# Last layer: first chunk's tiles side by side, products ahead of the mixture, second mixture first in a chunk

## The chip, the cores and the metric

The kernel runs on one core of one Trainium2 chip. The metric is the device time of one execution in microseconds (us). The kernel before took 3504.18 us as the median of 3 runs (3500.18 to 3504.94). PE is TensorE, DVE VectorE, ACT ScalarE, POOL GpSimd, SP the engine that issues the DMAs. Times of rows count from the start of the profiled execution's span.

## What is computed

Four residual layers on x of shape (16, 256, 512), 4096 tokens of width 512, all in fp32. The first three (a cross attention, a quantized feed-forward layer, a masked attention) are the same before and after. The fourth is the one that is touched:

```python
def _mole(x, W, b, A, Bm, Rw):
    gates = softmax(einsum('bsd,de->bse', x, Rw))          # 3 experts
    base = einsum('bsd,dh->bsh', x, W) + b
    z = einsum('bsd,edr->ebsr', x, A)                      # rank 8
    zg = z * transpose(gates, (2, 0, 1))[..., None]
    lora = einsum('ebsr,erh->bsh', zg, Bm)
    return base + SCALING * lora

def _L1_ffn_ref(x, W1, b1, A1, B1, R1, W2, b2, A2, B2, R2):
    h = relu(_mole(x, W1, b1, A1, B1, R1))                 # 512 -> 2048
    return _mole(h, W2, b2, A2, B2, R2)                    # 2048 -> 512

x = x + _L1_ffn_ref(_layernorm(x, axis=-1), ...)
```

## The kernel before

The last layer (`lora_ffn`, tile names `lf_`) works on the 4096 tokens in 8 chunks of 512. A chunk is four row tiles of 128 tokens. The engines' queues are written out by hand, one Python function for each engine, and they meet over semaphores. Every engine works through its queue in order, so what stands ahead of an instruction in its queue also holds it up.

**Products.** An fp32 factor is held as two parts, a high part rounded to fp32r and the rest, and `product` (L187 to L189) makes three matmuls of 128x128 by 128x512: high by high, high by low, low by high.

**Head of a chunk.** For each row tile `t`: SP loads it to `xin` (two buffers), DVE takes statistics (`stats`, L2473 and L2475), POOL makes the reciprocal deviation (L2462, L2464), DVE normalises the rows in place (`rows`, L2480), PE turns the tile with four transposes into the PSUM bank `pj` (`turn_tile`, L2644), ACT writes the high part of `xT` (`turned_hi`, L2570) and DVE the low part (`turned_lo`, L2485). There is one bank `pj`, and each job on it waits for the one before. When the four tiles are turned, PE makes the projections to gates and ranks (`first_projections`, eight matmuls, L2653), ACT copies them (`projected`, L2574, to `zT`), PE turns them back (`turn_projections`, L2660), DVE and ACT work out the gates and weigh the ranks (`mixture`, L2492 to L2516, with `exps`, L2578), PE turns the result (`turn_mixture`, L2667) and ACT copies it (`mixed`, L2582, to `mixT`).

**Body of a chunk.** `m` runs over 16 strips of 128 hidden features and two more steps (`LAG` is 2). In step `m` PE makes the strip's twelve main products and the side product with `mixT` (`hidden`, L187 to L189 and L2677) into one of two banks `hb`, ACT and DVE take the two parts of the relu from the bank (L2587, L2522), and two steps later PE uses the strip for the second product (`use_hidden`: two matmuls to `pz`, L2685, and twelve to the four banks `py`). Main products of strip `m` wait until the bank of strip `m - 2` has been read by DVE (`h_done`). The head of the next chunk lies within the body: tiles at `m` = 1 to 9, projections at 10, their turn at 11, the mixture's turn at 16.

**Tail of a chunk.** The second layer's projections of chunk `c - 1` (`pz`, copied by ACT at L2591 to `zT` as the last thing of its body) are handled inside the body of chunk `c`: the turn of the projections behind strip 0, `mixture` behind strip 0's low part on DVE, `exps` behind strip 0's high part on ACT, the turn of the mixture ahead of strip 2, and the side product and the output behind strip 2 (`second_lora`, L2698, `end`, L2528).

**Weights.** The two weight matrices are loaded in 16 pieces of 512 KB during chunk 0, in turn into the two halves of `y`. ACT and DVE split each (`piece_hi`, L2595; `piece_lo`, L2532). Piece `i` may be loaded when piece `i - 2` is split. Strips 0 and 1 need piece 0, strips 2 and 3 piece 1; the second product of strip 0 needs piece 2. Pieces 0 to 3 stand in the head of chunk 0, one behind each row tile, on both engines; piece `m + 4` stands in step `m` of the body. On SP the loads of tiles 2 and 3 of chunk 0 stand between the loads of pieces 1, 2 and 3 and wait until tile 0 or 1 has been turned and read (L2412, L2421).

**Start.** POOL clears `zg` with three memsets before anything else; DVE and PE wait for them first.

## Time and profile before

| | us |
|---|---|
| median of 3 runs | 3504.18 |
| lowest and highest run | 3500.18, 3504.94 |
| the profiled execution | 3504.39 |
| its span, first to last instruction | 3502.7 |
| PE busy in the span | 3225.8 (92%) |
| DVE, ACT, POOL busy | 1919.8, 1557.3, 779.3 |
| last layer, from its first instruction (2581.1) to the span's end | 921.6 |

The profile is one execution. The chain that ended last is PE's through nearly all of the last layer. A matmul's record is longer than the distance to the next one, since matmuls are pipelined; distances are taken between starts. "Granted clock" is the share of full speed that TensorE's throttle gave: 1.00 is 2.4 GHz, 0.50 is 1.2 GHz.

### The profile page before, as it was taken

To read this page: it belongs to the slowest core of one execution; us is meant where nothing else is said; L and a number is where in the kernel's file an instruction comes from. 1 tells how busy PE (TensorE), PEld (TensorE's weight loads), DVE (VectorE), ACT (ScalarE), POOL (GpSimd) and SP (SyncE) were. 2 spreads that over 40 slices of the span, in tenths; PEclk is the share of its full clock that TensorE was granted. 3 is DMA by queue.
4 is the path that set the end of the run, shared out by engine and by line. 5 is a ranking of instruction groups with operands and counts; after the bars stand their busy time and mean duration, and the time that the engine had idled before them with its cause. 6 is when DMAs were issued, how large, how long until landed. Compare 5 with 4: busy or idle time off the path is not lost. (4 is left out here: it accounts for less than half of the span.)

```text
span 3502.7 us, 51565 instructions
## 1 busy us (share of the span) xinstructions
PE 3225.8 (92%) x17304; PEld 2762.2 (79%) x17304; DVE 1919.8 (55%) x3294; ACT 1557.3 (44%) x2948; POOL 779.3 (22%) x1136
## 2 busy tenths in 40 slices
PE   7999979999999979998996787997959999999998
PEld 6989869999999967886885565885847777877776
DVE  3245558888888855556888885554743222122211
ACT  3222257777777743335776775654722111111110
POOL 0000057777777740000000200002710000000000
PEclk9999989999999999999998898998979999999999
DMA  6477754555555426555666675444832100011000
GB/s 184 134 238 235 220 171 148 153 156 165 154 153 159 144 95 243 177 174 174 221 221 218 208 235 200 166 168 148 253 103 84 37 31 19 24 36 37 31 25 12
DMA packets 370165, 503.48 MB, mean 144 GB/s; under 512 B 58940, under 2 KB 237420, under 8 KB 366032
## 3 DMA queue, kind: packets, MB, share of 16 engines
q1 hardware_dynamic: 356746, 475.46, 43.2%
q0 software_dynamic: 4480, 16.78, 1.4%
q10 hardware_dynamic: 8720, 8.41, 0.7%
q8 instruction: 127, 2.08, 0.3%
q14 instruction: 92, 0.75, 0.1%
HBM read 292.86 MB, written 174.11 MB: 133 GB/s over the span
## 5 line engine op out<-in xcount | busy, mean ns | idle before, releaser
L2522 DVE SCALAR_TENSOR_TENSOR lf_hT<-lf_hb,lf_hT 128x512 fp32r<-128x512 f32 x128 | 88.6, 692 | 618.8 <-ACT lf_hT L2587 617.4
L2587 ACT ACTIVATE lf_hT<-lf_hb 128x512 fp32r<-128x512 f32 x128 | 76.8, 600 | 685.1 <-PE lf_py L189 636.4
L770 POOL TENSOR_TENSOR at_prob<-at_prob,at_rec 128x308 f32<-128x308 f32 (+1 forms) x256 | 261.4, 1043 | 199.1 <-DVE at_rec L812 198.9
L906 ACT ACTIVATE at_prob<-at_sc,at_nm 128x77 f32<-128x77 f32 (+1 forms) x1024 | 293.5, 383 | 3.3 <-DVE at_nm L799 3.3
L799 DVE TENSOR_REDUCE at_nm<-at_sc 128x4 f32<-128x308 f32 (+1 forms) x256 | 164.8, 686 | 82.4 <-PE at_sc L960 80.8
L919 ACT ACTIVATE at_pT<-at_tp 128x1024 fp32r<-128x1024 f32 x128 | 131.8, 1030 | 166.7 <-PE at_tp L970 166.6
L187 PE MATMUL lf_hb<-lf_xT,lf_w 128*128 128x512 f32 x512 | 204.8, 400 | 0.0
L189 PE MATMUL lf_hb<-lf_xT,lf_w 128*128 128x512 f32 x512 | 203.7, 398 | 0.0
L189 PE MATMUL lf_py<-lf_w,lf_hT 128*128 128x512 f32 x512 | 203.2, 397 | 0.0
L188 PE MATMUL lf_hb<-lf_xT,lf_w 128*128 128x512 f32 x512 | 203.1, 397 | 0.0
L187 PE MATMUL lf_py<-lf_w,lf_hT 128*128 128x512 f32 x512 | 202.8, 396 | 0.0
L188 PE MATMUL lf_py<-lf_w,lf_hT 128*128 128x512 f32 x512 | 202.3, 395 | 0.0
L187 PE MATMUL dn_py<-qf_wd,dn_om 128*128 128x512 f32 x384 | 150.7, 393 | 25.2 <-DVE dn_om L1874 25.2
L805 DVE TENSOR_REDUCE at_sums<-at_prob 128x4 f32<-128x308 f32 (+1 forms) x256 | 172.9, 676 | 0.0
L816 DVE TENSOR_TENSOR at_pT<-at_tp,at_pT 128x1024 fp32r<-128x1024 f32 x128 | 156.5, 1222 | 29.9 <-ACT at_pT L919 29.9
L187 PE MATMUL pg_bank<-pg_xs,qg_wg 128*128 128x512 f32 x384 | 153.0, 398 | 20.7 <-DVE pg_xs L1369 20.7
L757 POOL TENSOR_TENSOR at_ks<-at_kr,at_ks 128x512 fp32r<-128x512 f32 x128 | 165.3, 1292 | 16.1 <-ACT at_ks L913 16.1
L187 PE MATMUL pu_bank<-pu_xs,qu_wu 128*128 128x512 f32 x384 | 150.8, 393 | 17.4 <-DVE pu_xs L1369 16.9
L2462 POOL TENSOR_SCALAR lf_var<-lf_mv 128x1 f32<-128x1 f32 x32 | 7.1, 223 | 717.4 <-DVE lf_mv L2475 717.4
L187 PE MATMUL at_vq<-at_xT,xo_Wq 128*128 128x256 f32 x512 | 147.0, 287 | 19.3 <-DMA at_xT<-xn_parts 12.7
L187 PE MATMUL at_vq<-at_pT,at_vs 128*128 128x256 f32 x512 | 154.9, 303 | 0.2 <-DVE at_qst L824 0.2
L960 PEld LDWEIGHTS at_sc<-at_ks,at_qs 128*128 128x128 f32 x1024 | 140.4, 192 | 14.2 <-DMA at_qs<-at_qst 4.4
(324 smaller groups left out, 9510.0 us busy)
## 6 DMA issues: line engine op xcount, KB each, us to landing
at_kr<-k_rows SPq DMA_DIRECT2D x256, 128.0 KB, 2.9
at_qs<-at_qst SPq DMA_DIRECT2D x512, 64.0 KB, 2.1
raw_gate<-pg_stage SPq DMA_DIRECT2D x96, 256.0 KB, 2.0
pu_rg<-raw_gate SPq DMA_DIRECT2D x96, 256.0 KB
raw_up<-pu_stage SPq DMA_DIRECT2D x96, 256.0 KB, 2.1
om_raw<-raw_up SPq DMA_DIRECT2D x48, 512.0 KB, 4.3
dn_raw<-raw_up SPq DMA_DIRECT2D x48, 512.0 KB, 3.8
xn_parts<-pr_xturned SPq DMA_DIRECT2D x32, 512.0 KB, 4.8
```

Of the source, the lines that this page charges most:

```text
L187: pe.matmul(out, lh, rh, start=start, stop=False, **kw)
L188: pe.matmul(out, lh, rl, start=False, stop=False, **kw)
L189: return pe.matmul(out, ll, rh, start=False, stop=stop, **kw)
L757: pool.tensor_tensor(ks[:, n % NK, :, 1, :], kr[:, n % NKR], ks[:, n % NK, :, 0, :].bitcast(F32), ALU.subtract).then_inc(k_low, 1)
L770: ins = pool.tensor_tensor(prob[:, i, :, lo:hi], prob[:, i, :, lo:hi], rec[:, z, g, :].unsqueeze(2).broadcast_to([P, 2 * NTE, hi - lo]), A ...
L799: ins = dve.tensor_reduce(nm[:, n % 2, g, :], sc[n % 2][:, :, lo:hi], AX_X, ALU.max, negate=True)
L805: dve.tensor_reduce(sums[:, z, g, :], prob[:, i, :, SEG[g][0]:SEG[g][1]], AX_X, ALU.add).then_inc(sum_done, 1)
L816: dve.tensor_tensor(pT[:, n % 2, 1], tp[:], pT[:, n % 2, 0].bitcast(F32), ALU.subtract).then_inc(pt_done, 1)
L906: ins = act.activation(prob[:, i, m, lo:hi], sc[n % 2][:, m, lo:hi], ACT.Exp, bias=nm[:, n % 2, g, m:m + 1])
L919: act.activation(pT[:, n % 2, 0], tp[:], ACT.Copy).then_inc(pt_hi, 1)
L960: ins = pe.matmul(sc[n % 2][:, h * NTE + m, :], qs[:, n % NQ, h, m * P:(m + 1) * P], ks[:, n % NK, h, part, :], start=part == 0, stop=part ...
L2522: dve.scalar_tensor_tensor(hT[:, i, 1, :], hb[i][:], 0.0, hT[:, i, 0, :].bitcast(F32), ALU.max, ALU.subtract).then_inc(h_done, 1)
```

## The change

Three edits, all in `lora_ffn`.

1. Chunk 0's four row tiles get a place each (`first_rows`: the two `xin` buffers, `zT` and `zg`, which are not in use yet) and a semaphore each for tiles 2 and 3. SP issues the four loads first and then those of pieces 0 to 3. DVE's order is statistics of two tiles, then rows, statistics and low parts overlapped; pieces 0 to 3 are split behind the tiles, except that piece 0 stands between tiles 1 and 2. PE turns each tile into a bank of its own (`py`, not in use yet). POOL's memsets of `zg` come after the four deviations and the four turns, and DVE waits for them only ahead of the first mixture.
2. `hidden` is cut into `hidden_main` (twelve products) and `hidden_side` (the product with `mixT`). In chunk 0 the main products of strip 0 stand behind the projections, those of strip 1 behind the turn of the projections; both side products follow the turn of the mixture.
3. In chunks 1 to 7 the turn of the second projections stands ahead of strip 0 on PE, `mixture` ahead of strip 0's low part on DVE and `exps` ahead of its high part on ACT.

```diff
--- before.py
+++ after.py
@@ -2357,6 +2357,9 @@
         w_high, w_low = ph.sem("w_high"), ph.sem("w_low")
         W1, W2 = a["L1_ffn_W1"], a["L1_ffn_W2"]
         PIECES, EARLY, PC = 2 * (KH // 2), 4, 2 * P
+        first_ready = [ph.sem(f"first_ready{i}") for i in range(2, NT)]
+
+        first_rows = [xin[:, 0, :], xin[:, 1, :], zT[:], zg[:].rearrange("p t n -> p (t n)")]
         block = ph.block()
 
 
@@ -2421,12 +2424,10 @@
                 sp.dma_start(staged(i), piece(i)[0]).then_inc(w_ready[i % 2], 16)
 
             head(0, range(2))
-            load_piece(0)
-            load_piece(1)
-            head(0, (2,))
-            load_piece(2)
-            head(0, (3,))
-            load_piece(3)
+            for t in range(2, NT):
+                sp.dma_start(first_rows[t], x3[t * P:(t + 1) * P, :]).then_inc(first_ready[t - 2], 16)
+            for i in range(EARLY):
+                load_piece(i)
             for i in range(EARLY, PIECES):
                 load_piece(i)
                 if i - EARLY in (0, 1, 3, 5):
@@ -2452,37 +2453,44 @@
 
         @block.gpsimd
         def _(pool):
-            pool.memset(zg[:], 0.0).then_inc(cleared, 1)
-            pool.wait_ge(cleared, 1)
-            pool.memset(zg[:, :, ROWH + ER:ROWH + ER + 1], 1.0).then_inc(cleared, 1)
-            pool.memset(zg[:, :, ROWL + ER:ROWL + ER + 1], 1.0).then_inc(cleared, 1)
-            with pool.Fori(0, NCH) as c:
+            def deviations(c):
                 for t in range(NT):
                     wait_alone(pool, mv_ready, NT * c + t + 1, spacer_p)
                     pool.tensor_scalar(var[:, t % 2:t % 2 + 1], mv[:, t % 2, 1:2], EPS, None, ALU.add).then_inc(var_done, 1)
                     pool.wait_ge(var_done, NT * c + t + 1)
                     pool.tensor_tensor(rstd[:, t % 2:t % 2 + 1], var[:, t % 2:t % 2 + 1], neghalf[:, 0:1], ALU.pow).then_inc(rstd_ready, 1)
 
+            deviations(0)
+            pool.wait_ge(pj_full, NT)
+            pool.memset(zg[:], 0.0).then_inc(cleared, 1)
+            pool.wait_ge(cleared, 1)
+            pool.memset(zg[:, :, ROWH + ER:ROWH + ER + 1], 1.0).then_inc(cleared, 1)
+            pool.memset(zg[:, :, ROWL + ER:ROWL + ER + 1], 1.0).then_inc(cleared, 1)
+            with pool.Fori(1, NCH) as c:
+                deviations(c)
+
         @block.vector
         def _(dve):
-            dve.wait_ge(cleared, 3)
-
-            def stats(c, t):
+            def stats(c, t, src=None):
                 i = t % 2
-                dve.wait_ge(x_ready[i], 32 * c + 16 * (t // 2) + 16)
-                dve.bn_stats(st[:, i, :], xin[:, i, :]).then_inc(stat_done, 1)
+                if src is None or t < 2:
+                    dve.wait_ge(x_ready[i], 32 * c + 16 * (t // 2) + 16)
+                else:
+                    dve.wait_ge(first_ready[t - 2], 16)
+                dve.bn_stats(st[:, i, :], xin[:, i, :] if src is None else src).then_inc(stat_done, 1)
                 wait_alone(dve, stat_done, NT * c + t + 1, spacer_d)
                 dve.bn_aggr(mv[:, i, :], st[:, i, :]).then_inc(mv_ready, 1)
 
-            def rows(c, t):
+            def rows(c, t, src=None):
                 i = t % 2
+                x = xin[:, i, :] if src is None else src
                 dve.wait_ge(rstd_ready, NT * c + t + 1)
-                dve.tensor_scalar(xin[:, i, :], xin[:, i, :], mv[:, i, 0:1], rstd[:, i:i + 1], ALU.subtract, ALU.mult).then_inc(xn_ready, 1)
-
-            def turned_lo(c, t, par):
+                dve.tensor_scalar(x, x, mv[:, i, 0:1], rstd[:, i:i + 1], ALU.subtract, ALU.mult).then_inc(xn_ready, 1)
+
+            def turned_lo(c, t, par, bank=pj):
                 cols = slice(t * P, (t + 1) * P)
                 dve.wait_ge(pj_hi, NT * c + t + 1)
-                dve.tensor_tensor(xT[:, par, 1, :, cols], pj[:].rearrange("p (k n) -> p k n", k=KD), xT[:, par, 0, :, cols].bitcast(F32),
+                dve.tensor_tensor(xT[:, par, 1, :, cols], bank[:].rearrange("p (k n) -> p k n", k=KD), xT[:, par, 0, :, cols].bitcast(F32),
                                   ALU.subtract).then_inc(pj_done, 1)
 
             def mixture(c, layer, job):
@@ -2531,21 +2539,32 @@
                 dve.wait_ge(w_high, i + 1)
                 dve.tensor_tensor(piece(i)[2], staged(i), piece(i)[1].bitcast(F32), ALU.subtract).then_inc(w_low, 1)
 
+            stats(0, 0, first_rows[0])
+            stats(0, 1, first_rows[1])
+            for s in x_ready:
+                dve.sem_inc(s, 16)
             for t in range(NT):
-                stats(0, t)
-                rows(0, t)
-                turned_lo(0, t, 0)
-                piece_lo(t)
+                rows(0, t, first_rows[t])
+                if t + 2 < NT:
+                    stats(0, t + 2, first_rows[t + 2])
+                if t >= 2:
+                    turned_lo(0, t - 2, 0, py[t - 2])
+            piece_lo(0)
+            turned_lo(0, 2, 0, py[2])
+            turned_lo(0, 3, 0, py[3])
+            for i in range(1, EARLY):
+                piece_lo(i)
+            dve.wait_ge(cleared, 3)
             mixture(0, 0, head_base(0) + NT + 1)
 
             def body(c, par, tail, nxt):
                 for m in range(KH + LAG):
+                    if tail and m == 0:
+                        mixture(c - 1, 1, tail_base(c - 1))
                     if m < KH:
                         hidden_lo(c, m)
                     if not tail and m + EARLY < PIECES:
                         piece_lo(m + EARLY)
-                    if tail and m == 0:
-                        mixture(c - 1, 1, tail_base(c - 1))
                     if tail and m == 1:
                         end(c - 1)
                     if nxt:
@@ -2565,9 +2584,9 @@
         def _(act):
             act.sem_inc(h_used, 2)
 
-            def turned_hi(c, t, par):
+            def turned_hi(c, t, par, bank=pj):
                 act.wait_ge(pj_full, head_base(c) + t + 1)
-                act.activation(xT[:, par, 0, :, t * P:(t + 1) * P], pj[:].rearrange("p (k n) -> p k n", k=KD), ACT.Copy).then_inc(pj_hi, 1)
+                act.activation(xT[:, par, 0, :, t * P:(t + 1) * P], bank[:].rearrange("p (k n) -> p k n", k=KD), ACT.Copy).then_inc(pj_hi, 1)
 
             def projected(job):
                 act.wait_ge(pj_full, job + 1)
@@ -2594,21 +2613,25 @@
                 act.wait_ge(w_ready[i % 2], 16 * (i // 2 + 1))
                 act.activation(piece(i)[1], staged(i), ACT.Copy).then_inc(w_high, 1)
 
-            for t in range(NT):
-                turned_hi(0, t, 0)
-                piece_hi(t)
+            turned_hi(0, 0, 0, py[0])
+            turned_hi(0, 1, 0, py[1])
+            piece_hi(0)
+            turned_hi(0, 2, 0, py[2])
+            turned_hi(0, 3, 0, py[3])
+            for i in range(1, EARLY):
+                piece_hi(i)
             projected(head_base(0) + NT)
             exps(0, 0)
             mixed(head_base(0) + NT + 2, 0)
 
             def body(c, par, tail, nxt):
                 for m in range(KH + LAG):
+                    if tail and m == 0:
+                        exps(c - 1, 1)
                     if m < KH:
                         hidden_hi(c, m)
                     if not tail and m + EARLY < PIECES:
                         piece_hi(m + EARLY)
-                    if tail and m == 0:
-                        exps(c - 1, 1)
                     if tail and m == 1:
                         mixed(tail_base(c - 1) + 1, 1)
                     if nxt:
@@ -2629,7 +2652,6 @@
         def _(pe):
             pe.sem_inc(z_done, 1)
             pe.sem_inc(h_done, 2)
-            pe.wait_ge(cleared, 3)
 
             def pj_free(job):
                 pe.wait_ge(pj_done, job + 1)
@@ -2642,6 +2664,12 @@
                 pj_free(head_base(c) + t)
                 for k in range(KD):
                     ins = pe.transpose(pj[:, k * P:(k + 1) * P], xin[:, t % 2, k * P:(k + 1) * P], ident[:])
+                ins.then_inc(pj_full, 1)
+
+            def turn_first(t):
+                pe.wait_ge(xn_ready, t + 1)
+                for k in range(KD):
+                    ins = pe.transpose(py[t][:, k * P:(k + 1) * P], first_rows[t][:, k * P:(k + 1) * P], ident[:])
                 ins.then_inc(pj_full, 1)
 
             def first_projections(c, par):
@@ -2667,14 +2695,16 @@
                     ins = pe.transpose(pj[:, t * P:(t + 1) * P], zg[:, t, :], ident[:])
                 ins.then_inc(pj_full, 1)
 
-            def hidden(c, m, par):
+            def hidden_main(c, m, par):
                 pe.wait_ge(h_done, KH * c + m + 1)
                 cols = slice(m * P, (m + 1) * P)
                 for k in range(KD):
                     product(pe, hb[m % 2][:], (w1[:, 0, k, cols], w1[:, 1, k, cols]), (xT[:, par, 0, k, :], xT[:, par, 1, k, :]), k == 0, False)
+
+            def hidden_side(c, m):
                 if m == 0:
                     pj_taken(head_base(c) + NT + 2)
-                pe.matmul(hb[m % 2][:], lb1[:, cols], mixT[:, 0, :], start=False, stop=True).then_inc(h_full, 1)
+                pe.matmul(hb[m % 2][:], lb1[:, m * P:(m + 1) * P], mixT[:, 0, :], start=False, stop=True).then_inc(h_full, 1)
 
             def use_hidden(c, u):
                 i = u % 2
@@ -2698,23 +2728,28 @@
                     pe.matmul(py[t][:], mixT[:, 1, t * P:(t + 1) * P], lb2[:], start=False, stop=True).then_inc(y_full, 1)
 
             for t in range(NT):
-                turn_tile(0, t)
+                turn_first(t)
             first_projections(0, 0)
+            pe.wait_ge(w_low, first_layer(0) + 1)
+            hidden_main(0, 0, 0)
             pj_taken(head_base(0) + NT)
             turn_projections(head_base(0) + NT + 1)
+            hidden_main(0, 1, 0)
             turn_mixture(0, 0, head_base(0) + NT + 2)
 
             def body(c, par, tail, nxt):
                 for m in range(KH + LAG):
+                    if tail and m == 0:
+                        pe.wait_ge(z_done, c + 1)
+                        turn_projections(tail_base(c - 1))
                     if m < KH:
                         if tail and m == 2:
                             turn_mixture(c - 1, 1, tail_base(c - 1) + 1)
                         if not tail and m % 2 == 0:
                             pe.wait_ge(w_low, first_layer(m) + 1)
-                        hidden(c, m, par)
-                    if tail and m == 0:
-                        pe.wait_ge(z_done, c + 1)
-                        turn_projections(tail_base(c - 1))
+                        if tail or m >= 2:
+                            hidden_main(c, m, par)
+                        hidden_side(c, m)
                     if tail and m == 2:
                         second_lora(c - 1)
                     if nxt:
```

## Rows read from the trace of the kernel before

**Rows 1.** The page's first line.

```profile
span 3502.7 us, 51565 instructions
```

**Rows 2.** Busy time by stretch: stretch, length, busy us (x instructions) PE, PEld, DVE, ACT, POOL, clock, DMA.

```profile
2581.00:2609.20 28.20, 4.43 (x16) 2.86 (x16) 11.86 (x19) 6.00 (x8) 3.88 (x11) 0.50 0.46 140
...
2626.10:2733.50 107.40, 101.64 (x438) 80.72 (x437) 33.56 (x55) 23.38 (x34) 3.15 (x8) 0.98 0.21 69
...
2841.90:2950.20 108.30, 107.28 (x478) 86.46 (x477) 25.63 (x62) 14.15 (x26) 3.16 (x8) 1.00 0.09 30
```

**Rows 3.** Timeline, layer's start: start us, duration, engine, line, operation, [idle before <- releaser].

```profile
2581.21 0.84 SPq L2412 DMA_DIRECT2D lf_xin<-x  x2
...
2584.05 0.69 DVE L2473 BATCH_NORM_STATS2 lf_st<-lf_xin 128x6 f32<-128x512 f32 x1 [10.11 <-DMA lf_xin<-x]
2584.89 0.18 DVE L2475 BATCH_NORM_AGGREGATE lf_mv<-lf_st 128x2 f32<-128x6 f32 x1
...
2586.24 0.55 DVE L2480 TENSOR_SCALAR lf_xin<-lf_xin,lf_mv,lf_rstd 128x512 f32<-128x512 f32 x1 [1.17 <-POOL lf_rstd L2464]
...
2588.01 0.60 ACT L2570 ACTIVATE lf_xT<-lf_pj 128x512 fp32r<-128x512 f32 x1 [21.17 <-PE lf_pj L2644]
2588.51 1.05 ACT L2595 ACTIVATE lf_w<-lf_y 128x1024 fp32r<-128x1024 f32 x1
2588.64 0.69 DVE L2485 TENSOR_TENSOR lf_xT<-lf_pj,lf_xT 128x512 fp32r<-128x512 f32 x1 [1.85 <-ACT lf_xT L2570]
...
2589.59 1.23 DVE L2532 TENSOR_TENSOR lf_w<-lf_y,lf_w 128x1024 fp32r<-128x1024 f32 x1 [0.25 <-ACT lf_w L2595]
```

**Rows 4.** The same timeline, from the projections to the first mixture's turn.

```profile
2609.21 3.42 PE L2653 MATMUL lf_pj<-lf_xT,lo_ra 128*128 128x512 f32 x8 [1.41 <-DVE lf_xT L2485]
...
2614.08 0.39 DVE L2492 COPY lf_z<-lf_pj 128x224 f32<-128x224 f32 x1 [3.44 <-PE lf_pj L2660]
...
2617.24 1.12 PE L2667 MATMUL lf_pj<-ident,lf_zg 128*128 128x128 f32 x4 [3.20 <-DVEq L2516]
```

**Rows 5.** DMA issues (KB, us to landing): of piece 0, then of piece 2.

```profile
lf_y<-in_L_ffn_W_dram SPq DMA_DIRECT2D x1, 512.0 KB, 6.0
...
lf_y<-in_L_ffn_W_dram SPq DMA_DIRECT2D x1, 512.0 KB, 3.8
```

**Rows 6.** Timeline: strip 0's side product, its parts on ACT and DVE, strip 2.

```profile
2622.83 0.40 PE L2677 MATMUL lf_hb<-lf_mixT,lo_lb 128*128 128x512 f32 x1
...
2623.26 0.60 ACT L2587 ACTIVATE lf_hT<-lf_hb 128x512 fp32r<-128x512 f32 x1 [4.27 <-PE lf_hb L2677]
...
2623.89 0.69 DVE L2522 SCALAR_TENSOR_TENSOR lf_hT<-lf_hb,lf_hT 128x512 fp32r<-128x512 f32 x1 [6.77 <-ACT lf_hT L2587]
...
2626.10 0.39 PE L187 MATMUL lf_hb<-lf_xT,lf_w 128*128 128x512 f32 x1
```

**Rows 7.** Timeline across the first of the seven chunk starts.

```profile
2731.16 0.60 ACT L2591 ACTIVATE lf_zT<-lf_pz 128x512 f32<-128x512 f32 x1 [3.02 <-PE lf_pz L2685]
...
2733.76 0.39 PE L187 MATMUL lf_hb<-lf_xT,lf_w 128*128 128x512 f32 x1
...
2736.80 0.60 PE L2660 MATMUL lf_pj<-ident,lf_zT 128*128 128x128 f32 x4
...
2740.04 0.40 PE L2677 MATMUL lf_hb<-lf_mixT,lo_lb 128*128 128x512 f32 x1
...
2741.46 0.66 PE L2667 MATMUL lf_pj<-ident,lf_zg 128*128 128x128 f32 x4 [1.02 <-DVEq L2516]
```

**Rows 8.** List of PE's waits, 2733.5 to 3500: us in total, times, longest.

```profile
PE lf_pj L2667 <- DVEq L2516: 10.3, 8, 3.2
```

**Rows 9.** Busy time by stretch again, 2 us each; the clock is the third from the end.

```profile
2612.00:2614.00 2.00, 1.22 (x7) 0.61 (x5) 0.00 (x0) 0.60 (x1) 0.00 (x0) 0.99 1.05 344
...
2616.00:2618.00 2.00, 0.76 (x4) 0.76 (x5) 1.02 (x7) 0.00 (x0) 0.00 (x0) 0.50 0.00 0
...
2622.00:2624.00 2.00, 2.00 (x10) 1.64 (x8) 0.11 (x1) 0.74 (x2) 0.00 (x0) 0.93 0.00 0
```

## The prediction

> **What bounds the kernel now.** I read the page's first line first [rows 1]: the span is 3502.7 us, the run around it 3504.39, so 1.69 us lie outside the span and I leave them as they are. The change touches only the last layer (names `lf_`), from about 2581 us to the end, so I next read busy time by stretch [rows 2]. In a middle chunk (2841.9 to 2950.2) PE works 107.28 of 108.30 us: time comes only from its waits or its order, and here just 1.02 us a chunk is to be had. The first chunk's body (2626.1 to 2733.5) has 5.76 us without PE work. The stretch ahead of it, 2581 to 2609.2, has 4.43 us of PE work in 28.2 us: a chain of small steps, one row tile after another. So there are two places to cost: the start of the layer, where the chain over DMA, DVE, POOL, PE and ACT sets the time, and the seven later chunk starts, where PE waits for the second mixture.
>
> **The start of the layer before.** One tile and one weight piece [rows 3]: DVE statistics (2584.05), aggregate to 2585.07 (1.02 for the two), 1.17 until the normalised row starts (2586.24, the deviation on POOL lies between), 0.55 for that row, 1.22 from its end to ACT's copy of the turned tile (PE's transposes lie between), 0.60 for the copy, DVE's low part 0.63 after the copy's start and 0.69 long, and then the piece that stands in the same queues ahead of the next tile's statistics: ACT 1.05, DVE 1.23, to 2590.82. The first low part ends at 2589.33, the fourth just ahead of PE's projections at 2609.21 [rows 4], so a tile with its piece takes 19.8 / 3 = 6.6 us.
>
> **The start after the change.** I lay the new queue orders out with the same durations. The first tile's statistics still start at 2584.05, since its load is still issued first. DVE: statistics and aggregate 0 to 2585.07, of tile 1 to 2586.11, row 0 to 2586.79 (its start, 2586.24, is bound by POOL as before), statistics 2 to 2587.82, row 1 2587.84 to 2588.39, statistics 3 to 2589.43, row 2 to 2590.00, low part 0 to 2590.71, row 3 to 2591.28, low part 1 to 2591.99. PE and ACT run beside it: tile 1 is turned from 2588.44 and copied by 2590.2. Then weight piece 0 (p0) is in both queues. Its load was issued right behind those of two row tiles (2581.21 + 0.84 and 0.06 [rows 3]) and took 6.0 us [rows 5]; now two more tiles, 0.5 MB, are ahead of it. No row has four tiles in flight, so I bound this: nothing more (landed at 2588.1), or once more the whole 2.8 us of a tile's load, 2581.21 to 2584.05 (2590.9). I take 2590.2, nearer to the later end, since the page counts bytes and these are 0.5 MB more. ACT converts it to 2591.35 and copies tiles 2 and 3 by 2593.1; DVE finishes p0 at 2593.24 and low parts 2 and 3 at 2594.66. PE's projections start at 2594.7 instead of 2609.21: 14.5 us. The late bound of p0 takes 0.2 off and the early one adds 0.1, because DVE is full until 2591.99 either way. Should tiles 2 and 3 themselves land a whole 2.8 us after their predecessors, row 3 would be some 1.5 us later; I keep that in the range.
>
> **From there to the third strip of products.** The eight projections ran at half clock, 3.42 us [rows 4]: to 2598.1. Now the 12 main products of strip 0 follow at once (p0 is ready), half a clock at first, to about 2601.3; before they stood behind the mixture. The next step is not PE's: ACT's copy of the projections (zT) stands behind the conversions of pieces 1 to 3. Piece 3 may load only when piece 1 is done: 2594.66 plus 1.25 on DVE, 0.1 to issue, 3.8 to land [rows 5], 1.05 on ACT: 2600.9, and with 0.65 for the copy 2601.5. So the wait for the load of piece 3 is what is late next. Turning zT starts at 2601.6 and takes 0.7; DVE, which finishes piece 3 at 2602.1, begins the mixture at 2602.3; 3.16 us from its first instruction (2614.08) to PE's turn of the result (2617.24) [rows 4] give 2605.5. Strip 1's 12 products, 2.8 us, are done by then. The mixture's turn and copy (0.66 at full clock [rows 7] and 0.60) end at 2606.8, and the two side products follow. Here stands a new wait: strip 2 needs the bank of strip 0, whose chain begins only with the side product. ACT starts 0.43 after it (2623.26 against 2622.83), DVE 0.63 later, 0.69 long [rows 6]: strip 2 starts at about 2608.7. Before, strip 1's products covered this and strip 2 began at 2626.10 [rows 6]. Gain to that point: 17.4 us. From both sides: 15.1 (late tiles 1.5, p0 0.2, pieces 2 and 3 in each other's way 0.6) to 18.3 (loads of pieces 0.3 shorter, new waits 0.6 smaller).
>
> **The rest of chunk 0** keeps its order on all engines. Its PE waits, within the 5.76 us of [rows 2], come from row tiles of chunk 1 behind weight pieces, and all of these are paced by the strips, so the whole stretch moves with strip 2 and costs the same. Pieces 4 and 5 come early enough (issued 2599.6 and 2602.4, used from 2608 on). I count 0, between 1 us lost (piece 5 and strip 1's second half now queue closer together on ACT and DVE) and 1 us gained.
>
> **POOL and SP at the start.** Three memsets move behind POOL's four deviations and behind the fourth turn; DVE's and PE's wait for them leaves the start of both queues, and DVE's now stands ahead of the mixture, 9 us later: nothing. SP's loads of tiles 2 and 3 no longer wait for a turned tile between pieces. Two more semaphores are to be cleared at the end: taken as 0.1 us, inside the rounding.
>
> **The seven chunk starts.** Before: strip 0, turn of the second projections (2736.80), strip 1 whose last product starts at 2740.04, and the turn of the mixture at 2741.46 [rows 7]. Products are 0.233 apart (thirteen from 2733.76 to 2736.80), so PE was free at 2740.27 and lost 1.19 us; the profile puts it at 1.02 because it models ends. The first of the seven is shown, the list of waits has 10.3 us for the eight second mixtures, the longest, 3.2, being the very last [rows 8]: 7.1 for the seven. After: the turn stands first, at 2733.76, DVE starts behind its 0.60, and the result is ready 3.16 later, 2737.6; PE arrives there after the turn and 26 products, 6.1 us, at 2740.2. It is covered with 2.6 us to spare, and nothing queued behind on PE waits. Strip 0's ACT and DVE steps now stand behind the mixture on DVE and the exponential on ACT; they are wanted at strip 2, so this costs nothing. zT's copy runs 2731.16 to 2731.76 [rows 7], 2.0 us ahead of the moved turn. So 7 x 1.19 = 8.3, with 7 x 1.02 = 7.1 as the lower bound; I take 8.2. The last mixture after chunk 7 is not covered before or after: 0.
>
> **Sum.** 17.4 + 8.2 = 25.6 us. 3504.39 less 25.6 is 3478.8; against the median 3504.18, which is 0.2 lower, 3478.6. I say 3478.7.
>
> **Rivals.**
> (a) The clock falls in the new start. In the trace PE's granted clock was 0.99 (2.4 GHz) between 2612 and 2614, fell to 0.50 (1.2 GHz) by 2616 after PE had waited 3.20 us of the mixture, and only came back to 2.4 GHz at about 2622.3 [rows 4, 9]; so some 4.3 us of strip 0 were at half speed, with 3.42 / 8 = 0.43 a product instead of 0.233: ten products, 1.9 us lost. Now PE waits 0.3, 0.5, 0.7 and 1.1 us between 2601 and 2609, with work between. If these waits together bring the clock down again, strips 0 to 2 cost 2 to 4 us more: 3480.7 to 3482.7. For it: PE works about 4 of those 7.4 us. Against it: each wait is much shorter than the 3.20. The Trainium skill, page "TensorE: Matmul & The Clock Gate", section "HAM oscillation", has PE go back to half rate between bursts when it idles; the trace agrees with the fall after 3.20 us and does not show what several short waits do. Chance 0.15.
> (b) Weights bound chunk 0. Piece 4 is issued only about 4.5 us earlier than before (2599.6 against 2590.82 + 2 x 6.6 = 2604.0), while strip 2 is 17.4 earlier. If the stream of pieces sets the pace of the body, the start's gain shrinks to 4.5: 3504.4 - 4.5 - 8.2 = 3491.7. Against it: from piece 6 on the stream waits for the strips, not they for it. Chance 0.06.
> (c) The second mixture is not covered, and the start is right: 3504.4 - 17.4 = 3487.0. It would be so if DVE began the mixture over 2.6 us late. Chance 0.03.
> (d) Slower. The moved turn waits for zT at the head of PE's queue with all of strip 0 behind it. Up to 2.0 us after 2731.76 this is free; beyond that each microsecond costs 7. The break-even of the whole change is a copy later by 2.0 + 8.2/7 + 17.4/7 = 5.7 us; at 6.2 the kernel is 3.8 us slower, 3508.2. Against it: ACT idled before that copy and nothing is added ahead of it. Chance 0.02.
>
> **How the numbers follow.** Forecast 0.74, (a) 0.15, (b) 0.06, (c) 0.03, (d) 0.02. The forecast's own bounds: 15.1 + 7.1 - 1.0 = 21.2 to 18.3 + 8.3 + 1.0 = 27.6, or 3476.8 to 3483.2; the three runs shown spread over 4.8 us, so I widen by 1.3 on both sides, which takes in (a) whole: 3475.5 to 3484.5. Within 0.2% (7 us) is about what a measurement of this kernel can tell from no change. All cases but (d) are faster by more; I leave 0.02 for the same: faster 0.96, same 0.02, slower 0.02.
>
> **What would show it.** PE's projections start 13.5 us after the layer's first load is issued instead of 28.0; strip 2 some 27.5 instead of 44.9; the idle time before the mixture's turn, 1.02 in seven places, is gone and the chunk period is 107.1 instead of 108.3; the idle time before the very last one stays 3.2. A period of 108.3 makes the second part wrong; a start at 2594.7 with chunk 1 not 17 us earlier makes (b) right; a granted clock under 0.9 after 2602 makes (a) right.

## The result

The changed kernel took 3474.81 us (median of 4 runs, 3470.35 to 3476.10), the kernel before 3503.55 beside it (4 runs, 3500.18 to 3504.94): ratio 0.9918, 95% interval 0.9903 to 0.9934, 28.7 us faster. The forecast was 3478.7, range 3475.5 to 3484.5: the direction is right, and the median lies 0.7 us below the range. Four more runs of the same kernel (below) gave 3478.1 beside 3503.19: ratio 0.9930 (0.9913 to 0.9946), 25.1 us.

The page's first line, after:

```profile
span 3472.1 us, 51566 instructions
```

Busy time by stretch, after. The stretches answer to those of [rows 2]: first load to projections, strip 2 to PE's first work on chunk 1, one middle chunk.

```profile
2578.20:2590.90 12.70, 4.46 (x16) 2.86 (x16) 8.72 (x18) 4.17 (x6) 4.19 (x11) 0.50 0.53 168
...
2605.40:2711.00 105.60, 100.34 (x438) 79.77 (x439) 34.62 (x56) 23.30 (x35) 3.15 (x8) 1.00 0.21 70
...
2711.00:2818.10 107.10, 107.10 (x478) 86.59 (x477) 25.80 (x62) 14.01 (x26) 3.16 (x8) 1.00 0.09 30
```

Much the same PE work (4.46 us, 4.43 before) now lies in 12.7 us instead of 28.2. The middle chunk is 107.1 us long and has no time without PE work left. But the stretch between them, whose order was not touched, is shorter too, 105.6 instead of 107.4, and its clock is 1.00 where [rows 2] has 0.98. That is the surprise. Measured between two events, from strip 2's first product to ACT's copy of the second projections, it is 103.07 instead of 105.06, 2.0 us less.

The start, after (answers to [rows 3]):

```profile
2578.43 0.84 SPq L2415 DMA_DIRECT2D lf_xin<-x  x2
...
2581.17 0.69 DVE L2480 BATCH_NORM_STATS2 lf_st<-lf_xin 128x6 f32<-128x512 f32 x1 [9.99 <-DMA lf_xin<-x]
2582.01 0.18 DVE L2482 BATCH_NORM_AGGREGATE lf_mv<-lf_st 128x2 f32<-128x6 f32 x1
2582.11 0.66 DVE L2480 BATCH_NORM_STATS2 lf_st<-lf_xin 128x6 f32<-128x512 f32 x1
...
2583.36 0.55 DVE L2488 TENSOR_SCALAR lf_xin<-lf_xin,lf_mv,lf_rstd 128x512 f32<-128x512 f32 x1 [0.26 <-POOL lf_rstd L2461]
2583.82 0.69 DVE L2480 BATCH_NORM_STATS2 lf_st<-lf_zT 128x6 f32<-128x512 f32 x1
...
2586.97 1.05 ACT L2614 ACTIVATE lf_w<-lf_y 128x1024 fp32r<-128x1024 f32 x1
...
2588.45 1.22 DVE L2540 TENSOR_TENSOR lf_w<-lf_y,lf_w 128x1024 fp32r<-128x1024 f32 x1
...
2589.59 1.28 DVE L2493 TENSOR_TENSOR lf_xT<-lf_py,lf_xT 128x512 fp32r<-128x512 f32 x2
```

DVE has hardly a gap from tile to tile. An instruction that need not wait starts about 0.08 us before the recorded end of the one before (2582.11 against 2582.19). Piece 0 is there when ACT reaches it (2586.97, no wait in brackets).

From the projections to strip 2, after (answers to [rows 4] and [rows 6]):

```profile
2590.92 3.78 PE L2681 MATMUL lf_pj<-lf_xT,lo_ra 128*128 128x512 f32 x8 [1.82 <-DVE lf_xT L2493]
...
2596.39 0.58 ACT L2593 ACTIVATE lf_zT<-lf_pj 128x512 f32<-128x512 f32 x1
...
2598.10 0.60 PE L2688 MATMUL lf_pj<-ident,lf_zT 128*128 128x128 f32 x4
...
2601.97 0.66 PE L2695 MATMUL lf_pj<-ident,lf_zg 128*128 128x128 f32 x4 [0.48 <-DVEq L2524]
...
2603.41 0.70 PE L2707 MATMUL lf_hb<-lf_mixT,lo_lb 128*128 128x512 f32 x2 [0.78 <-ACT lf_mixT L2601]
...
2605.38 0.47 PE L187 MATMUL lf_hb<-lf_xT,lf_w 128*128 128x512 f32 x1 [1.27 <-DVE lf_hT L2530]
```

The three short waits of PE are those of the prediction: 0.48 for the mixture, 0.78 for its copy, 1.27 for strip 0's bank.

The first of the seven chunk starts, after (answers to [rows 7]):

```profile
2708.45 0.60 ACT L2610 ACTIVATE lf_zT<-lf_pz 128x512 f32<-128x512 f32 x1 [3.02 <-PE lf_pz L2715]
...
2711.04 0.60 PE L2688 MATMUL lf_pj<-ident,lf_zT 128*128 128x128 f32 x4
...
2711.68 0.39 DVE L2500 COPY lf_z<-lf_pj 128x224 f32<-128x224 f32 x1 [6.01 <-PE lf_pj L2688]
...
2714.59 0.26 DVE L2522 TENSOR_TENSOR lf_zg<-lf_zf,lf_zg 128x96 fp32r<-128x96 f32 x1
...
2717.54 0.60 PE L2695 MATMUL lf_pj<-ident,lf_zg 128*128 128x128 f32 x4
```

The mixture ends at 2714.85, PE comes to its turn at 2717.54 and has nothing to wait for.

**Where the time went**, between the two profiles: the unchanged three layers 2.8 us (first load issued at 2578.43 instead of 2581.21); first load to strip 2 17.9 (26.95 instead of 44.89); strip 2 to the copy of chunk 0's last products on ACT 2.0 (103.07 instead of 105.06); seven chunks 8.6; and 0.7 lost at the very end. Together 30.6, the difference of the spans. Of the last item 0.1 is SP's clearing of two more semaphores, 0.055 us each; the rest is PE's clock: the final turn of a mixture is the same work behind the same 3.20 us wait, once at full and once at half clock (before, then after):

```profile
3491.23 0.66 PE L2667 MATMUL lf_pj<-ident,lf_zg 128*128 128x128 f32 x4 [3.20 <-DVEq L2516]
```

```profile
3459.93 1.11 PE L2695 MATMUL lf_pj<-ident,lf_zg 128*128 128x128 f32 x4 [3.20 <-DVEq L2524]
```

The 2.0 us of chunk 0 are mostly of the same kind. In the kernel before PE waited 2.35 us for a row tile of chunk 1 and went on at 2651.58; then its clock fell for a few microseconds. Products by PE's timeline, and the clock by stretch of 2 us (third from the end), of before:

```profile
2653.84 0.63 PE L188 MATMUL lf_py<-lf_w,lf_hT 128*128 128x512 f32 x1
2654.26 0.63 PE L189 MATMUL lf_py<-lf_w,lf_hT 128*128 128x512 f32 x1
```

```profile
2652.00:2654.00 2.00, 2.00 (x10) 1.63 (x8) 0.00 (x0) 0.00 (x0) 0.00 (x0) 0.75 0.03 8
2654.00:2656.00 2.00, 2.00 (x7) 1.52 (x6) 0.00 (x0) 0.00 (x0) 0.00 (x0) 0.50 0.00 0
2656.00:2658.00 2.00, 2.00 (x9) 1.64 (x8) 0.22 (x1) 0.85 (x2) 0.00 (x0) 0.89 0.00 0
```

Some eight products 0.43 instead of 0.233 apart: 1.6 us. The waits in the stretch are 0.5 us shorter too (5.3 instead of 5.8). In the profile of after the waits at the same places (4.7 us in four, the two long ones 1.98 and 2.01 us instead of 2.35 and 2.14) are followed by no such fall. Whether that is the change's doing or chance had to be tried.

### The profile page after: what moved, and what is told of

The parts are those of the page before. It is cut to its first block and busy times, and to the rows that moved or that the text cites. A ratio compares the mean times of both kernels' runs of the same rounds, so it can differ in the third digit from the quotient of the medians.

```text
span 3472.1 us, 51566 instructions
## 1 busy us (share of the span) xinstructions
PE 3220.1 (93%) x17304; PEld 2757.9 (79%) x17304; DVE 1918.3 (55%) x3294; ACT 1552.7 (45%) x2948; POOL 777.9 (22%) x1136
## 5 line engine op out<-in xcount | busy, mean ns | idle before, releaser
L757 POOL TENSOR_TENSOR at_ks<-at_kr,at_ks 128x512 fp32r<-128x512 f32 x128 | 165.3, 1291 | 13.8 <-ACT at_ks L913 13.8
L187 PE MATMUL at_vq<-at_xT,xo_Wq 128*128 128x256 f32 x512 | 146.8, 287 | 16.8 <-DMA at_xT<-xn_parts 12.6
```

The lines of the kernel that those rows point to most:

```text
L187: pe.matmul(out, lh, rh, start=start, stop=False, **kw)
L757: pool.tensor_tensor(ks[:, n % NK, :, 1, :], kr[:, n % NKR], ks[:, n % NK, :, 0, :].bitcast(F32), ALU.subtract).then_inc(k_low, 1)
```

## The experiments

All times "after the first load" count from SP's first issue in the last layer, so that the unchanged layers drop out. "Rest of chunk 0" is from strip 2's first product to ACT's copy of the second projections. The period is the mean of the seven chunks from that copy to the last one (the last chunk has no head of a next one in it, so it is below the 108.3 of a middle chunk).

| kernel | median, us | before beside it | projections | strip 2 | rest of chunk 0 | falls in it | period |
|---|---|---|---|---|---|---|---|
| before | 3503.55 | | 28.0 | 44.9 | 105.06 | 1 | 107.66 |
| before again | 3499.01 (1 run) | 3502.43 | 28.1 | 45.0 | 107.01 | 2 | 107.66 |
| edit 3 alone | 3493.21 | 3502.43 | 28.0 | 44.8 | 106.30 | 2 | 106.43 |
| edit 1 alone | 3489.30 | 3502.43 | 12.6 | 31.1 | 106.37 | 2 | 107.71 |
| edits 1 and 2 | 3488.00 | 3502.43 | 12.6 | 26.5 | 108.48 | 3 | 107.70 |
| after | 3474.81 | 3503.55 | 12.5 | 26.95 | 103.07 | 0 | 106.44 |
| after again | 3478.10 | 3503.19 | 12.4 | 26.6 | 108.50 | 3 | 106.43 |
| row tiles first | 3468.68 | 3503.19 | 12.5 | 26.7 | 99.02 | 1 | 106.43 |
| start kept busy | 3476.77 | 3503.19 | 12.5 | 26.0 | 106.75 | 2 | 106.47 |
| all moves | 3461.72 | 3503.19 | 11.9 | 23.9 | 99.01 | 1 | 106.44 |
| waits filled | 3473.87 | 3500.69 | 12.5 | 26.9 | 105.35 | 1 | 106.44 |
| all filled | 3463.77 | 3500.69 | 11.9 | 23.9 | 97.49 | 0 | 106.43 |

A "fall" is a stretch in which PE works at a granted clock of 0.50 in the profile.

**Edit 3 alone.** The kernel before with the second mixture first, shown for PE:

```diff
+                    if tail and m == 0:
+                        pe.wait_ge(z_done, c + 1)
+                        turn_projections(tail_base(c - 1))
                     if m < KH:
...
                         hidden(c, m, par)
-                    if tail and m == 0:
-                        pe.wait_ge(z_done, c + 1)
-                        turn_projections(tail_base(c - 1))
```

> Edit 3 alone on the kernel before: in chunks 1 to 7 the turn of the second projections, the mixture and the exponential stand first. Theory (the wait of 1.02 to 1.04 us by the profile is 1.2 us of lost PE time, seven times): chunk period 107.1 instead of 108.3, the layer 8.4 to 8.7 us shorter, 3495 us against 3503.5, ratio 0.9976. Rival (the list of waits is the price: 7.1 us): period 107.3 and 3496.4. Rival (the start of the layer and edit 3 depend on each other): a period other than 107.1 here while it is 107.1 with all three edits. The start up to strip 2 stays 44.9 us after the first load's issue. If the clock's fall at the third wait of chunk 0 is a matter of where that wait falls in time, it may be there or not: strip 2 to the end of chunk 0's products takes 105.1 with it and 103.5 without.

Measured: ratio 0.9973 (0.9963 to 0.9982) over 10 runs, 9.2 us by the medians. The period fell by 1.23, in seven chunks 8.6 us: the first theory, not the 7.1 of the list of waits. That list now has one wait left for a second mixture, the final one:

```profile
PE lf_pj L2667 <- DVEq L2516: 3.2, 1, 3.2
```

The clock fell twice in the rest of chunk 0, which this edit doesn't reach.

**Edit 1 alone, and edits 1 and 2.** The changed kernel with the two or the one remaining edit undone. Edit 2 undone:

```diff
             first_projections(0, 0)
-            pe.wait_ge(w_low, first_layer(0) + 1)
-            hidden_main(0, 0, 0)
             pj_taken(head_base(0) + NT)
             turn_projections(head_base(0) + NT + 1)
-            hidden_main(0, 1, 0)
             turn_mixture(0, 0, head_base(0) + NT + 2)
...
-                        if tail or m >= 2:
-                            hidden_main(c, m, par)
+                        hidden_main(c, m, par)
```

> Edit 1 alone (four row tiles side by side, four banks, memsets later); the products of strips 0 and 1 stay behind the mixture, the second mixture stays behind strip 0. Theory: PE's projections start 12.5 us after the first load's issue instead of 28.0. The copy of the projections then waits for the conversion of piece 3 (1.7 us), so that strip 2 starts 44.9 - 15.5 + 1.7 = 31.1 us after it, a gain of 13.8: 3489.8 us. Rival (that copy does not matter): 29.4, gain 15.5. Rival (weights bound chunk 0): strip 2 early, but the end of chunk 0 only 4.5 us early, 3499. Chunk period 108.3.

> Edits 1 and 2: as the run with edit 1 alone, and the main products of strips 0 and 1 ahead of the mixture. Theory: strip 2 starts 27.0 us after the first load's issue, 17.9 less than before and 4.1 less than with edit 1 alone; chunk period 108.3; 3485.6 us. Rival (the products ahead of the mixture only move the wait): within 1 us of edit 1 alone.

Measured: edit 1 alone 0.9966 (0.9952 to 0.9980), strip 2 at 31.1, 13.8 us earlier, as the theory has it: PE waits 2.48 us for the copy of the projections, which comes after piece 3's conversion on ACT.

```profile
2594.77 1.06 ACT L2614 ACTIVATE lf_w<-lf_y 128x1024 fp32r<-128x1024 f32 x1 [1.07 <-DMA lf_y<-in_L_ffn_W_dram]
2595.74 0.58 ACT L2593 ACTIVATE lf_zT<-lf_pj 128x512 f32<-128x512 f32 x1
...
2596.46 0.63 PE L2688 MATMUL lf_pj<-ident,lf_zT 128*128 128x128 f32 x4 [2.48 <-ACT lf_zT L2593]
```

The rest of chunk 0 is 106.37, between the 105.06 and 107.01 of the kernel before. A stream of weights that gave back only 4.5 of the 13.8 us would have stretched it by 9.3: rival (b) of the prediction is out. With edit 2, strip 2 is at 26.5, 4.6 us earlier again, but the medians differ by only 1.3 us (ratio 0.9958, 0.9941 to 0.9974). The two profiled spans are even the same, 3487.6: in the run with edit 2 the rest of chunk 0 was 2.1 longer, with three falls of the clock instead of two, and the layers ahead of it, which neither edit touches, were 3.3 longer. The total alone would not tell edit 2 from nothing; strip 2's place does.

**The kernel before again, and the changed one again**, both without an edit:

> The kernel before once more, for a second profile. Theory A: the 2.0 us by which the rest of chunk 0 was longer in the profile of before than in that of after are mostly one fall of PE's clock, nine products at 0.43 instead of 0.233 apart after the 2.35 us wait for a row tile, and whether it comes is a matter of chance: in another profile of the same kernel the clock can stay at 1.00 there and the stretch from strip 2 to the last products' copy takes 103.5 instead of 105.06. Theory B: it belongs to the kernel before, and is there again (105.06).

> The changed kernel once more, for a second profile and more runs. In the profiles so far PE's clock fell in the rest of chunk 0 (after strip 2) once and twice with the kernel before, twice and three times with parts of the change, and not at all in the profile of the changed kernel; each fall lasts about 3.4 us and costs 1.6. Theory A (chance): here one to three falls, the stretch from strip 2 to the copy of the last products 104.6 to 108.5 instead of 103.07, strip 2 again 26.5 to 27.0 us after the first load's issue, chunk period 107.1. Theory B (the change does away with the falls): 103.1 again.

The changed kernel gave theory A: 108.50 with three falls, where its first profile had 103.07 and none. The kernel before gave 107.01 with two falls, which neither theory had. The fall behind its first long wait came again, as theory B says, and one came behind the second, where the first profile had none. So the change does not do away with the falls, and their number varies in both kernels; that the kernel before can be without any is not shown. Clock by stretch, after again, around strip 2 (at 2603.6), and behind its two longest waits:

```profile
2603.60:2606.00 2.40, 2.39 (x7) 1.93 (x8) 2.29 (x3) 1.52 (x3) 0.00 (x0) 0.65 0.03 7
2606.00:2608.00 2.00, 2.00 (x6) 1.58 (x6) 1.46 (x3) 0.00 (x0) 0.20 (x1) 0.57 0.63 241
...
2632.00:2634.00 2.00, 2.00 (x6) 1.63 (x5) 0.00 (x0) 0.00 (x0) 0.00 (x0) 0.50 0.03 8
...
2650.00:2652.00 2.00, 2.00 (x6) 1.59 (x5) 0.00 (x0) 0.00 (x0) 0.00 (x0) 0.50 0.24 93
```

The first pair is rival (a) of the prediction: after waits of 0.5, 0.8 and 1.3 us PE goes to half clock in strip 2. Nine of the twelve profiles fit one count within 0.3 us: rest of chunk 0 = 97.7 + PE's waits in it + 1.6 for each fall (before 97.7 + 5.7 + 1.6 = 105.0; after 97.7 + 5.2 = 102.9; after again 97.7 + 6.0 + 4.8 = 108.5; added matmuls counted as work). The three with the row tiles first are 0.7 to 0.8 below it; they have four stops of PE fewer, and by the chunk starts (1.19 lost against 1.02 listed) a stop costs some 0.2 more than the list has.

**Row tiles first.** Chunk 0 on DVE:

```diff
+                    if not tail and m in (2, 4, 6, 8):
+                        rows(c + 1, m // 2 - 1)
                     if not tail and m + EARLY < PIECES:
                         piece_lo(m + EARLY)
...
-                        if m in (2, 4, 6, 8):
+                        if tail and m in (2, 4, 6, 8):
                             rows(c + 1, m // 2 - 1)
```

> The changed kernel with one more edit: in steps 2, 4, 6 and 8 of chunk 0 DVE normalises the row tile of chunk 1 ahead of splitting a weight piece. Theory: PE's four waits for row tiles there (4.7 us, the longest 2.0) go, and with them every fall of the clock after strip 2, so that the stretch from strip 2 to the last copy is 98.3 to 98.9 against 103.07 without and up to 108 with falls; 4.7 us off a profile without falls, up to 9.5 off one with three; time 3474.8 - 6 = 3469. Rival (the falls have nothing to do with these waits): 4.7 us off and still one to three falls. Rival (the pieces then come late for the products): PE waits for weights instead, less than 2 us gained.

Measured: 0.9906 (0.9890 to 0.9923), 3468.68, against 3478.10 of the changed kernel beside it. In the two profiles the rest of chunk 0 is 9.5 us shorter, of which 5.5 are waits and 3.2 two falls fewer; against the changed kernel's first profile, which had no fall, it is only 4.0 shorter (99.02, 103.07). The four waits are gone from the list, the falls behind them too; the one at strip 2 stays, which the theory had wrong ("every fall after strip 2").

```profile
2603.00:2605.00 2.00, 2.00 (x7) 1.64 (x6) 2.00 (x3) 1.19 (x2) 0.00 (x0) 0.63 0.03 8
...
2607.00:2701.70 94.70, 94.19 (x417) 75.82 (x416) 30.65 (x51) 21.24 (x31) 3.03 (x8) 1.00 0.23 73
```

PE does not wait for weights: the second rival is out.

**The start kept busy.** Matmuls added while PE waits, without use for the output:

```diff
+            def keep_busy(n):
+                for _ in range(n):
+                    pe.matmul(pj[:], lb1[:, 0:P], lb1[:, 0:CT], start=True, stop=True)
+
+            keep_busy(12)
             for t in range(NT):
                 turn_first(t)
+                keep_busy(3 if t < NT - 1 else 8)
             first_projections(0, 0)
```

> The changed kernel with 29 matmuls of 512 columns added on PE while it waits in the start (12 ahead of the first tile's turn, 3 between turns, 8 ahead of the projections), into the bank that the projections overwrite; they give nothing to the output. Theory (PE's clock, not its work, sets the stretch from the projections to the turn of zT): the eight projections take 2.0 us instead of 3.4 to 3.8, strip 0 has no product at half clock; the copy of the projections then waits for the conversion of piece 3 (done 18.0 us after the first load's issue), so the turn of zT starts at 18.6 instead of 19.7 and strip 2 at 26.0 instead of 26.95. Rival (weights and DVE set it): strip 2 within 0.2 us of 26.95. Rival (the added matmuls get in the way): projections later than 12.5.

Measured: projections in 2.11 us, turn of zT at 18.7, strip 2 at 26.0, as the theory has it. Now ACT's copy is late next, as the prediction had expected for the changed kernel itself:

```profile
2584.14 2.11 PE L2681 MATMUL lf_pj<-lf_xT,lo_ra 128*128 128x512 f32 x8 [0.44 <-DVE lf_xT L2493]
...
2590.33 0.63 PE L2688 MATMUL lf_pj<-ident,lf_zT 128*128 128x128 f32 x4 [1.27 <-ACT lf_zT L2593]
```

The median (3476.77, range 3469.68 to 3477.40) cannot show 1 us. PE's three short waits ahead of strip 2 are as before (0.46, 0.78 and 1.28 us), and yet no fall follows them here: the two falls of this profile are those behind the long waits.

**Waits filled.** The changed kernel with work in its two long waits of chunk 0:

```diff
             def turn_tile(c, t):
-                pe.wait_ge(xn_ready, NT * c + t + 1)
                 pj_free(head_base(c) + t)
+                if isinstance(c, int) and c == 1 and t in (1, 2):
+                    for _ in range(8):
+                        pe.matmul(pj[:], lb1[:, 0:P], lb1[:, 0:CT], start=True, stop=True)
+                pe.wait_ge(xn_ready, NT * c + t + 1)
```

> The changed kernel with eight matmuls of 512 columns added on PE ahead of its two long waits for row tiles in chunk 0 (2.0 to 2.5 us each), into a bank that is free and is overwritten by the turn; they give nothing to the output, and the waits themselves stay. The profiles so far fit this count for the stretch from strip 2 to the last copy: 97.7, plus PE's waits in it (5.2 to 6.0), plus 1.6 for each fall of the clock. Theory (it is PE's idleness in these waits that lets the clock fall some 50 and 70 us after the first load): no fall there, the stretch 103.1, or 104.7 if the clock falls at strip 2. Rival (the falls come from something else, so they stay): 106 to 108.5.

Measured: 105.35. Of it 3.7 are the 16 added matmuls and 2.3 the waits left. One fall, at strip 2, none behind the filled waits:

```profile
2605.00:2607.00 2.00, 2.00 (x6) 1.51 (x6) 1.77 (x3) 0.00 (x0) 0.00 (x0) 0.50 0.84 220
2607.00:2708.30 101.30, 98.96 (x433) 78.66 (x432) 30.88 (x51) 21.24 (x32) 3.16 (x8) 1.00 0.21 69
```

That is 0.6 over the expected 104.7; the tiles still come when they came, so the added work shortens nothing but PE's idle time. This speaks for PE's idleness as what brings the falls, not the row tiles or the weights. It is one profile, and the changed kernel's first one had no fall there either; together with the row tiles first it weighs more. All four profiles without a long idle wait in this stretch have no fall after the one at strip 2, and seven of the eight with such waits have one or two. The median (3473.87, ratio 0.9923) does not tell this version from the changed kernel.

**All moves, and all filled.** Row tiles first, the start kept busy, and pieces 0, 2 and 3 split later (shown for ACT); the second version adds eight matmuls in the three waits around the first mixture's turn:

```diff
             turned_hi(0, 1, 0, py[1])
-            piece_hi(0)
             turned_hi(0, 2, 0, py[2])
             turned_hi(0, 3, 0, py[3])
-            for i in range(1, EARLY):
-                piece_hi(i)
+            piece_hi(0)
+            piece_hi(1)
             projected(head_base(0) + NT)
             exps(0, 0)
+            piece_hi(2)
+            piece_hi(3)
             mixed(head_base(0) + NT + 2, 0)
```

```diff
             hidden_main(0, 1, 0)
+            keep_busy(2, pz)
             turn_mixture(0, 0, head_base(0) + NT + 2)
+            keep_busy(2, pz)
...
                         hidden_side(c, m)
+                        if not tail and m == 1:
+                            keep_busy(4, pz)
```

> A version meant to beat both: the changed kernel with the row tiles of chunk 1 ahead of the weight pieces on DVE, the 29 added matmuls, piece 0 split behind all four tiles, and pieces 2 and 3 split behind the copy of the projections on ACT and behind the first mixture on DVE. Theory: projections at 11.5 us, turn of zT at 16.3 instead of 19.7, strip 2 at 23.5 instead of 26.95; no fall of the clock after strip 2 and that stretch 98.5 instead of 103.07; together 8 us off the changed kernel's profile, 3466. Rival (with pieces 2 to 5 later, the weights become late in the first steps): strip 2 early, but new waits of PE for weights and at most 4 us gained.

> The version with all moves, with eight more added matmuls in PE's three waits around the first mixture's turn (two ahead of the turn, two behind it, four behind strip 1's side product), into a bank that is not in use yet. In the profile with all moves the clock fell at strip 2, 23.9 us after the first load, after waits of 0.5, 0.8 and 1.3 us. Theory (short waits close together let the clock fall): no fall at all from the start to the end of chunk 0, the stretch from strip 2 to the last copy 97.4 instead of 99.0, strip 2 still at 23.9; 3460.1 against 3461.7. Rival (the waits are too short to matter): the fall stays, 3461.7.

Measured: all moves 3461.72, ratio 0.9882 (0.9865 to 0.9898), strip 2 at 23.9 (0.4 later than expected, as the projections are), one fall there. It beats both kernels, the changed one by 16.4 us beside it. Of the 15.2 between those two profiled spans 9.5 are in the rest of chunk 0, where two falls of three and four waits are gone, 2.7 up to strip 2, and 3.5 in layers that are the same in both, less 0.4 at the end. The 8 us expected were off the changed kernel's first profile, and in the last layer alone 7.2 of them are there (893.6 less 886.4). All filled: no fall, clock 1.00 from the projections to the end of chunk 0, and strip 2 in the same place:

```profile
2587.00:2599.00 12.00, 11.34 (x52) 8.42 (x51) 7.76 (x18) 4.66 (x7) 0.00 (x0) 1.00 0.36 110
2599.00:2696.40 97.40, 96.89 (x428) 77.97 (x429) 34.53 (x56) 23.97 (x35) 3.17 (x8) 1.00 0.28 89
```

The fall at strip 2 is gone with the waits, as the theory has it. This too is one profile, and with the waits in place the fall came in five profiles of seven. The 1.5 us are there in the stage (97.49 against 99.01) but not in the medians (3463.77 beside 3500.69, ratio 0.9896, against 0.9882): which of the two versions is the faster is open.

## Why the prediction was right or wrong

**The start, right in size, partly by errors that cancel.** Forecast 17.4 up to strip 2, measured 17.9 and 18.4. Projections came at 12.5 instead of 13.5 after the first load: I had put DVE's instructions end to end by their durations with 0.02 between them, while one that need not wait starts some 0.08 before the recorded end of the last; over a dozen that is the 1.0 us. Tiles 2 and 3 and piece 0 came early enough, so the late bounds of the loads were not needed. Then I named the copy of zT behind piece 3 as what is late next; in the changed kernel it was PE itself, whose clock rose only at 2596, four products into strip 0, so that the turn of zT started 1.1 us after the copy's end. With a warm PE the copy is late next, by 1.3. The new wait for strip 0's bank was forecast at 1.1 and is 1.27.

**The seven chunk starts, right.** Forecast 1.19 each and 8.2 in all, measured 1.23 and 8.6, with edit 3 alone as with all three. The distance between starts was the right price, the listed wait (1.02) was not.

**The rest of chunk 0, the step that failed.** It was counted as 0 with 1 us on either side, because its order does not change. Measured it was 2.0 us shorter in the first pair of profiles and 1.5 longer in the second (107.01, 108.50). Its order does not change, but its time runs from 103.07 to 108.50 in one and the same kernel, by zero to three falls of the clock. The profile of before had one of them, and I read its 105.06 as fixed. I had the mechanism, as rival (a), only for the new start. It was at work behind most waits of 2 us in the stretch, before and after.

**The range, too narrow.** The first pair of profiles gained 30.6 us where the sum has 25.6. Of the 5.0 more, 2.8 are in the layers that the change leaves alone, for which the sum has no term, 2.0 in the rest of chunk 0, 0.5 in the start and 0.4 in the chunk starts, less 0.7 at the end. Only one of the four runs was profiled, so how much of each is in the median, which is 0.7 below the range, stays open; either of the first two is enough for it. The range was widened by 1.3 us for the spread of the runs, from three of them. The eight runs of the changed kernel lie between 3470.35 and 3480.83, with a median of 3476.0, those of the kernel before between 3496.69 and 3508.08. Two groups of four of the same kernel differ by 3.3 us in the median. The rest of chunk 0 gives up to 5.4 us of that (4.8 for three falls); the layers in front can give more: the first load of the last layer was issued at 2581.21 and 2574.09 in two profiles of the kernel before. The base of the sum, 3504.39, was one run from this spread, 1 to 4 us above the medians of 3500.69 to 3503.55 that larger groups gave. With the layer alone, 26.4 us by the two pairs of profiles (921.49 and 923.21 less 893.67 and 898.15), against the forecast 25.6, the sum was 0.8 short; each side has three falls in its two profiles, so the falls are not in this 0.8.

**Rivals.** (a) is right in some executions: the fall at strip 2 is in four of the five profiles that have edits 1 and 2 and no added work in the start, not in the first one of after. It costs 1.6, not 2 to 4. The argument against (a) was that each wait is much shorter than the 3.20 us after which the clock fell. But the clock did not hold until the end of that wait. It ran from 2614.04 to 2617.24; the clock fell before 2616, as the line below shows, and was at 0.50 from there [rows 9]:

```profile
2614.00:2616.00 2.00, 0.04 (x1) 0.00 (x0) 1.47 (x7) 0.21 (x1) 0.00 (x0) 0.87 0.06 21
```

So the row did not show that a wait has to be as long as 3.20 us.

(b), (c) and (d) are out: the rest of chunk 0 did not lengthen with the start's gain, the second mixture is covered, and the copy of zT was 2.0 us early (2709.05 against 2711.04).

## What to carry to other kernels

Price a wait that is to be removed by the distance between the starts of the instructions around it, and look in the profile for every place where the granted clock drops behind a wait, and put each into the range as a term that may or may not be there next time, even in stretches that the change leaves alone. A wait of 2 us on a busy TensorE can cost 1.6 us more than itself; moving one small instruction ahead of a large one in a queue (the row tile ahead of the weight piece) gained 9.4 us by the medians, a third of what the three edits had; 3.2 of it were two falls fewer in the profiles, which another pair of runs may not show. Where a gain is smaller than the spread of the runs, compare stages from a common event, not totals.

## What the runs showed of the hardware

A fall of the clock from 2.4 to 1.2 GHz cost 1.6 us of dense products. Eight profiles have two long waits of PE each in the rest of chunk 0, of 1.98 to 2.70 us. Thirteen of these sixteen were followed by a fall. The three that were not are of 1.98 and 2.01 us (both in the changed kernel's first profile) and of 2.14 us (in that of before), while one of 2.09 was. So the shortest were the ones without, but length alone does not decide. Behind the three waits of 0.5, 0.8 and 1.3 us within 4 us the clock fell in five profiles of seven. With matmuls without use put into the waits there was no fall, in one profile each (the two long waits, and those ahead of strip 2, which still began at 23.9). The Trainium skill, page "TensorE: Matmul & The Clock Gate", section "HAM oscillation", tells of PE idling between bursts and starting each at half rate; these runs agree in kind, with the clock rows of the changed kernel's second profile (0.57 at strip 2). What decides whether one and the same wait brings a fall stays open.
